# One block of sixteen of the first attention pass fetched by one-hot products; the second relational sum waits for the group it reads

## The chip, the cores and the metric

The kernel runs on one NeuronCore of a Trainium2 chip. The metric is device time in microseconds (us) of the whole program, lower is better. Five engines work side by side, each through its own list of instructions in order: TensorE (PE; its weight loads are shown as PEld), VectorE (DVE), ScalarE (ACT), GpSimd (POOL) and SyncE (SP), the last here only to issue DMAs. They meet through semaphores.

## The reference, cut to what matters

Four graph layers follow one another on 3125 nodes with 128 features and 100000 edges sorted by destination. Every layer is preceded by a layer norm with relu and added to `x`. The change touches the first layer, a graph attention with 8 heads, and the sum of the second layer (with which the edge half of the fourth is computed):

```python
# layer 0: attention over the incoming edges of each node
xl = (x @ W).reshape(N, 8, 16)
a_src, a_dst = (xl * att_src).sum(-1), (xl * att_dst).sum(-1)
e = leaky_relu(a_src[src] + a_dst[dst], 0.2)
ex = exp(e - segment_max(e, dst)[dst])
alpha = ex / (segment_sum(ex, dst)[dst] + 1e-16)
out = segment_sum(alpha[:, :, None] * xl[src], dst)

# layer 1, applied twice: a weight per relation
H = einsum("ni,rio->nro", x, einsum("rb,bio->rio", comp, V))
agg = segment_sum(H[src, etypes] * norm, dst)
```

So each edge needs the row of its source node: 128 features of `xl` and 8 numbers `a_src` in layer 0, and 128 features of its (node, relation) pair in layer 1.

## The kernel before

The edges, in order of destination, are cut into blocks of 128, two blocks to a "super" (391 supers). Destinations are cut into 25 tiles of 128 nodes. A step is one super for one tile; a super that straddles two tiles gets a step for each, so there are 415 steps, padded to 416. `ntile` and `estep`, computed on the chip, hold each step's tile and super. Four steps make a set, so there are 104 sets (`SETS`) of 8 blocks.

**The first attention pass**, `stage_gat` (calls from L653 on). POOL fetches one row of the table `tab0` (136 floats: `xl` and `a_src`) for each edge of a block with one indirect DMA, eight to a set, 832 in all (L691), into a ring `G` of `RG` = 12 sets; it may overwrite a set's place once DVE has weighted it (`y_done`). The iteration s of the main loop does this:

- ACT: `onehots(s+1)`, two operations over 1024 columns (L702, L705) on the destination numbers that SP has loaded to all partitions (`load_dst`, L657), giving the transposed one-hot matrix `MT`; `copy_weights(s-8)` (L713); one small step of the softmax (`step_of`: one of four steps in turn, so that four sets make one chunk of the softmax).
- PE: `score_products(s)` (L904, 8 products of 8 columns, each with a weight load of 128), `sums(s-8, 0)` (L947), the softmax step's transposes (L918 to L934), `sums(s-8, 1)`. The sums of a step go to one of `RS` = 5 PSUM banks.
- DVE: the softmax step (`masks`, `scans`, `chain`, `maxima`), `weigh(s-8)` (one-hots at L847, the product with the gathered rows at L855), `add_up(s-9)` (L840), `scores(s)` (L870, L873), which waits for the landing of all gathers of set s.

`LAG` = 8 sets lie between the scores and the weighted sums of a set. PE, ACT and DVE release each other within an iteration; POOL is only held by the ring. SP stands in its own queue: after two `load_dst` come three loads of single columns (L667 to L671), the first keys (L662), loads for a neighbouring stage (`aside.loads`), then `load_dst(2)` and so on.

**The last sum**, `stage_last_sum`, is not changed but has been using the method that the change brings to the first pass: one block in eight isn't fetched by POOL. Its source numbers are loaded to all partitions; for each of the 25 node tiles, ACT (two operations, L1111 and L1120) or DVE (one, L1165) builds a one-hot matrix of 128 nodes by 512 edges, PE multiplies it by the table's tile and adds up the 25 products (L1193), and the result, turned by four transposes (L1200), is copied into the ring.

**The second relational sum**, `stage_edges` (L477 on). POOL gathers 98 groups (`GROUPS_N`) of 8 blocks (L503, 782 gathers, the last group has 6) into a ring of 16 groups. PE makes the edge features (`features`, L535) and the sums (L555 for the gathered rows, L559 for the features), DVE adds them up (L595), ACT does relu and weights. Groups hold supers 4g to 4g+3, while set s holds steps 4s to 4s+3; because straddling supers take two steps, the super of a step falls behind the step's number, by 24 at the end. Before the change PE waits at set s < 98 for all of group s (`full[s % RG]`) whichever group its steps read.

## Time and profile before

| | us |
|---|---|
| three runs | 5646.87, 5653.91, 5638.48 |
| their median | 5646.87 |
| the profiled execution | 5653.79, of it 5652.1 in the span of the core |
| `stage_gat`, first gather to the last addition | 53.6 to 1178.5 |
| `stage_edges`, first gather to the last addition | 2356.7 to 3379.7 |
| `stage_last_sum`, first gather to the last | 4717.8 to 5586.2 |

| engine | busy over the span |
|---|---|
| POOL | 3887.6 us (69%) |
| PE | 3821.5 us (68%) |
| DVE | 2680.4 us (47%) |
| ACT | 2032.5 us (36%) |

Five of the program's stages are rows of indirect DMAs on POOL, one after the other. The busy share of an engine over the span tells little, since what an engine costs depends on the stage; the stretches of a stage and the waits within it have to be read. PE's clock is granted at one of two levels, 1.2 and 2.4 GHz, shown as 0.50 and 1.00; a mean between them is a mixture. The profiled execution is 6.9 us above the median of the three runs.

### The profile page before, as it was taken

The numbers are of one execution on the slowest core, as the hardware profiler recorded it, in microseconds if no ns is written. First come the engines' busy times: TensorE is split into PE (matmuls) and PEld (weight loads), VectorE is DVE, ScalarE is ACT, GpSimd is POOL, SyncE is SP. The second block draws the span as 40 slices with busy tenths as digits, with TensorE's granted clock in tenths as the row PEclk, the third lists the DMA queues.
The fourth block names the chain that finished last, engine by engine and source line by source line (L and its number), as shares of the span: only waits on it lengthen the run. The fifth ranks groups of instructions, "written<-read, shape, count | busy, mean of one in ns | idle before, by whom it ended". The sixth has DMA issues, their size and how long they took to land. (4 is left out here: it accounts for less than half of the span.)

```text
span 5652.1 us, 74589 instructions
## 1 busy us (share of the span) xinstructions
PE 3821.5 (68%) x20008; PEld 3215.9 (57%) x20008; DVE 2680.4 (47%) x8891; ACT 2032.5 (36%) x4370; POOL 3887.6 (69%) x4031
## 2 busy tenths in 40 slices
PE   3677777764533333777777776666676776988885
PEld 3676677743433333577777774665566663555554
DVE  4566666673222222433343344777777764332222
ACT  2222222220000000233333334566556636766663
POOL 6777777707777777477777744777777734777774
PEclk6555555577656556777777787999999988999997
DMA  4333334323222111422222215565665612222221
GB/s 124 108 108 105 108 107 110 100 89 106 53 54 52 52 52 52 140 60 60 60 60 60 60 39 161 159 160 158 160 159 158 159 50 65 62 60 60 60 58 42
DMA packets 393967, 515.71 MB, mean 91 GB/s; under 512 B 103179, under 2 KB 279138, under 8 KB 393178
## 3 DMA queue, kind: packets, MB, share of 16 engines
q0 software_dynamic: 128128, 265.50, 18.9%
q1 hardware_dynamic: 262745, 245.10, 14.5%
q8 instruction: 177, 2.90, 0.2%
q14 instruction: 228, 1.86, 0.1%
q10 hardware_dynamic: 2689, 0.36, 0.1%
HBM read 466.63 MB, written 43.94 MB: 90 GB/s over the span
## 5 line engine op out<-in xcount | busy, mean ns | idle before, releaser
L1696 POOL DMA_INDIRECT arena<-tab_x,idx_a x880 | 833.0, 947 | 314.5 <-issue 267.7
L996 POOL DMA_INDIRECT arena<-tab_rel,idx_b x782 | 761.8, 974 | 390.9 <-issue 238.2
L691 POOL DMA_INDIRECT arena<-tab,idx_a x832 | 821.0, 987 | 259.6 <-issue 252.5
L503 POOL DMA_INDIRECT arena<-tab_rel,idx_b x782 | 743.3, 951 | 267.9 <-issue 238.1
L1097 POOL DMA_INDIRECT arena<-tab_h,idx_a x686 | 660.5, 963 | 269.0 <-issue 208.5
L1037 PE MATMUL PS<-arena,att 128*128 x1664 | 359.4, 405 | 594.8 <-DMA arena<-tab_rel,idx_b 579.1
L1037 PEld LDWEIGHTS PS<-arena,att 128*128 128x128 f32 x1664 | 335.9, 309 | 619.4 <-issue 619.3
L1014 DVE TENSOR_SCALAR att<-iota_row,drel,wgt 128x128 f32<-128x128 f32 x832 | 222.9, 366 | 694.0 <-PE PS L1037 693.9
L1193 PE MATMUL PS<-arena,H 128*128 128x512 f32 x1200 | 538.6, 603 | 11.0 <-ACT arena L1134 11.0
L595 DVE TENSOR_TENSOR arena<-arena,PS 128x128 f32 x832 | 240.5, 289 | 601.5 <-PE PS L559 526.6
L555 PE MATMUL PS<-arena,att 128*128 x1664 | 372.2, 365 | 223.3 <-DMA arena<-tab_rel,idx_b 210.7
L947 PE MATMUL PS<-att,arena 128*128 128x136 f32 x1664 | 426.3, 435 | 62.1 <-issue 53.9
L555 PEld LDWEIGHTS PS<-arena,att 128*128 128x128 f32 x1664 | 323.5, 272 | 242.2 <-issue 241.4
L947 PEld LDWEIGHTS PS<-att,arena 128*128 128x128 f32 x1664 | 382.6, 325 | 70.0 <-issue 59.0
L1878 DVE SCALAR_TENSOR_TENSOR arena<-arena,att,PS 128x129 f32 x880 | 307.1, 349 | 215.4 <-issue 80.8
L1797 ACT ACTIVATE arena<-arena,att 128x128 f32<-128x128 f32 x880 | 281.2, 390 | 330.5 <-DVE att L1866 330.4
L1753 PE MATMUL PS<-arena 128*128 128x129 f32 x1760 | 267.3, 296 | 194.6 <-ACT arena L1789 194.6
L904 PEld LDWEIGHTS PS<-arena 128*128 128x128 f32 x1664 | 358.9, 325 | 56.5 <-issue 56.5
L904 PE MATMUL PS<-arena 128*128 x1664 | 348.0, 347 | 54.6 <-ACT arena L705 41.7
L1193 PEld LDWEIGHTS PS<-arena,H 128*128 128x128 f32 x1200 | 228.8, 196 | 273.1 <-issue 236.8
L1165 DVE TENSOR_SCALAR arena<-arena 128x512 f32<-128x512 int32 x192 | 101.1, 527 | 558.8 <-PE PS L1193 554.1
L1753 PEld LDWEIGHTS PS<-arena 128*128 128x128 f32 x1760 | 223.5, 198 | 250.5 <-ACT arena L1789 250.5
(389 smaller groups left out, 7209.9 us busy)
## 6 DMA issues: line engine op xcount, KB each, us to landing
arena<-pair_d SPq DMA_DIRECT2D x220, 256.0 KB
arena<-tab_u SPq DMA_DIRECT2D x880, 64.0 KB
arena<-drel_rows SPq DMA_DIRECT2D x104, 512.0 KB
tab_rel<-arena SPq DMA_DIRECT2D x50, 512.0 KB
arena<-tab_rel,idx_b POOLq DMA_INDIRECT x1564, 2.5
arena<-tab_x,idx_a POOLq DMA_INDIRECT x880
arena<-tab,idx_a POOLq DMA_INDIRECT x832
arena<-tab_h,idx_a POOLq DMA_INDIRECT x686
```

The costliest lines, as they stand in the source:

```text
L503: pool.indirect_dma_start(out=G[:, o:o + D], out_offset=None, in_=table, in_offset=bass.IndirectOffsetOnAxis(ap=idx_row[:, c:c + 1], axis= ...
L555: nc.tensor.matmul(PS[:, b:b + D], MW[s % 2][:, k * P:(k + 1) * P], G[:, bass.ds(e * (2 * D) + g * D, D)], start=(g == 0), stop=(g == 1))
L691: pool.indirect_dma_start(out=G[:, o:o + 136], out_offset=None, in_=tab0, in_offset=bass.IndirectOffsetOnAxis(ap=idx_src[:, 8 * s + k:8 * ...
L904: ins = nc.tensor.matmul(B7[:, k * 8:k * 8 + 8], MT[s % 2][:, k * P:(k + 1) * P], ad[:, bass.ds(tiles[k // 2] * 8, 8)], start=True, stop=True)
L947: ins = nc.tensor.matmul(PS[:, b:b + W], M[s % 2][:, k * P:(k + 1) * P], Y[s % 2][:, k, :, :].rearrange("p h c -> p (h c)"), start=(g == 0 ...
L996: pool.indirect_dma_start(out=G[:, o:o + D], out_offset=None, in_=table, in_offset=bass.IndirectOffsetOnAxis(ap=idx_row[:, c:c + 1], axis= ...
L1037: ins = nc.tensor.matmul(acc, M[s % RM][:, k * P:(k + 1) * P], G[:, bass.ds(e * (2 * D) + g * D, D)], start=False, stop=True, skip_group_c ...
L1097: pool.indirect_dma_start(out=G[:, o:o + D], out_offset=None, in_=table, in_offset=bass.IndirectOffsetOnAxis(ap=idx_last[:, c:c + 1], axis ...
L1193: nc.tensor.matmul(BANK, H[:, c * D:(c + 1) * D], SEL[i % NS], start=(c == 0), stop=(c == NT - 1)).then_inc(pick_done, 1)
L1696: pool.indirect_dma_start(out=G[:, o:o + D], out_offset=None, in_=tab_x, in_offset=bass.IndirectOffsetOnAxis(ap=idx_pair[:, 4 * g + u:4 * ...
L1753: ins = nc.tensor.matmul(PS[:, b:b + W], PB_[g % 2][:, u * P:(u + 1) * P], G[:, o:o + W], start=True, stop=True)
L1878: dve.scalar_tensor_tensor(a, a, ff[g % 8][:, u:u + 1], PS[:, b:b + W], ALU.mult, ALU.add).then_inc(acc_done, 1)
```

## The change

In `stage_gat`, from set 8 on, the last block of every second set (s odd, `picked(s)`) is no longer gathered: 48 blocks, one of sixteen, so POOL issues 784 gathers. Four such blocks (512 edges) of eight sets are made together, one quad ahead. In iteration s of an eight, up to four of the 25 node tiles are dealt with (4, 4, 4, 4, 4, 4, 1, 0): ACT builds the one-hot matrix for 17 of the 25 tiles with `distance` and `select`, DVE for 8, in one of four buffers `SEL`, and PE multiplies it by the table's tile in `X` after the iteration's sums (`pick`). In the eighth iteration ACT copies the result out of PSUM (`rows_out`), PE turns it (`turn`), ACT copies it again (`rows_back`), and `row_in(s+2)` puts a block in its place in the ring. DVE computes that block's `a_src` itself in `scores`, with a product and a reduction. There are 12 quads and 300 picks.

The table stays in `X`: at the end of `stage_begin` ACT copies `xl` there, and SP loads `x` back at the end of `stage_gat`. The buffers `SEL` and `SRC` lie in `H`, which SP first stores to `tab_h` and loads back at the end. PSUM bank 4 goes to the picks, so `RS` is 4. The source numbers are stored in `src_rows` by `stage_begin`.

In `stage_edges` POOL announces each group's landing through one counter, `landed`: after the third gather of group g it waits until group g-1 has landed and adds one. PE waits at set s for the number of groups that its last step needs, `need[s] = (estep[4s+3] >> 2) + 1`, computed on DVE.

```diff
@@ stage_edges
+                            if g and c == 8 * g + 2:
+                                pool.wait_ge(full[(g - 1) % RG], 128 * ((g - 1) // RG + 1))
+                                pool.sem_inc(landed, 1)
+                    last = GROUPS_N - 1
+                    pool.wait_ge(full[last % RG], 128 * (last // RG) + 16 * (2 * ST - 8 * last))
+                    pool.sem_inc(landed, 1)
...
+                        groups = load_need(mybir.EngineType.PE, need, s)
                         pe.wait_ge(r_done, s + 1)
                         pe.wait_ge(w_done, s + 1)
-                        if s < GROUPS_N:
-                            pe.wait_ge(full[s % RG], 128 * (s // RG) + 16 * min(8, 2 * ST - 8 * s))
+                        pe.wait_ge(landed, groups)
@@ stage_begin, ACT and SP
+                    sp.dma_start(src_rows.rearrange("(b p) e -> p b e", p=JB),
+                                 sl[1][0:JB, :].rearrange("p (b e) -> p b e", b=4)).then_inc(s_rows, 16)
...
+                    act.wait_ge(s_ev, 7)
+                    nc.scalar.copy(v3(X[:]), tab[:, :, 0:D])
@@ stage_gat
-            RS, W = 5, 136
+            RS, W = 4, 136
...
+            def picked(s):
+
+                return s >= 8 and s % 2 == 1
...
+            def chunks(s):
+
+                q, v = s // 8 + 1, s % 8
+                return [(q, c) for c in range(min(4 * v, NT), min(4 * v + 4, NT))] if q < QUADS else []
@@ stage_gat, SP
                     load_key(0)
                     load_key(1)
+                    sp.dma_start(tab_h.rearrange("(t p) f -> p t f", p=P), v3(H[:])).then_inc(s_keep, 16)
+                    sp.wait_ge(s_keep, 16)
+                    load_src(1)
+                    load_src(2)
                     aside.loads(sp)
                     for s in range(2, SETS):
                         sp.wait_ge(mt_done, s - 1)
                         load_dst(s)
+                        if s % 8 == 1 and 3 <= s // 8 + 1 < QUADS:
+                            q = s // 8 + 1
+                            sp.wait_ge(sel_act, NA * (q - 2))
+                            sp.wait_ge(sel_dve, ND * (q - 2))
+                            load_src(q)
...
                     aside.stores(sp)
+                    sp.wait_ge(pick_done, NT * (QUADS - 1))
+                    sp.wait_ge(sel_act, NA * (QUADS - 1))
+                    sp.dma_start(v3(X[:, 0:(NT - 1) * D]), node_view(t["x"], True)).then_inc(s_keep, 16)
+                    sp.dma_start(X[0:NLAST, (NT - 1) * D:NW], node_view(t["x"], False)).then_inc(s_keep, 16)
+                    sp.dma_start(v3(H[:]), tab_h.rearrange("(t p) f -> p t f", p=P)).then_inc(s_keep, 16)
+                    sp.wait_ge(s_keep, 64)
@@ stage_gat, POOL
-                        for k in range(8):
+                        for k in range(7 if picked(s) else 8):
@@ stage_gat, ACT
+                    def distance(j):
+
+                        q, c = j // NA + 1, ACT_TILES[j % NA]
+                        if j % NA == 0:
+                            act.wait_ge(s_src[q % 2], 16 * ((q + 1) // 2))
+                        if j >= 2:
+                            act.wait_ge(sel_act, j - 1)
+                        nc.scalar.activation(DIST[j % 2], SRC[q % 2], ACT.Abs, bias=away[:, c:c + 1]
+                                             ).then_inc(dist_done, 1)
+
+                    def select(j):
+
+                        i = NT * (j // NA) + ACT_TILES[j % NA]
+                        act.wait_ge(dist_done, j + 1)
+                        if i >= NS:
+                            act.wait_ge(pick_done, i - NS + 1)
+                        nc.scalar.activation(SEL[i % NS], DIST[j % 2], ACT.Relu, bias=ones[:, 0:1], scale=-1.0
+                                             ).then_inc(sel_act, 1)
@@ stage_gat, DVE
                     def scores(s):
...
+                        if picked(s):
+                            n = s // 2 - 3
+                            dve.wait_ge(made, n)
+                            dve.tensor_tensor(WS, g[:, 7, 0:D], asb, ALU.mult).then_inc(s_ws, 1)
+                            dve.wait_ge(s_ws, 2 * n - 1)
+                            dve.tensor_reduce(g[:, 7, D:D + 8], WS.rearrange("p (h c) -> p h c", c=16), AX_X, ALU.add
+                                              ).then_inc(s_ws, 1)
+                            dve.wait_ge(s_ws, 2 * n)
@@ stage_gat, PE
+                    def pick(q, c):
+
+                        i = NT * (q - 1) + c
+                        if c in DVE_TILES:
+                            pe.wait_ge(sel_dve, ND * (q - 1) + DVE_TILES.index(c) + 1)
+                        else:
+                            pe.wait_ge(sel_act, NA * (q - 1) + ACT_TILES.index(c) + 1)
+                        if c == 0 and q > 1:
+                            pe.wait_ge(freed, q - 1)
+                        nc.tensor.matmul(BANK, X[:, c * D:(c + 1) * D], SEL[i % NS], start=(c == 0), stop=(c == NT - 1)
+                                         ).then_inc(pick_done, 1)
...
                         if s >= LAG:
                             sums(s - LAG, 1)
+                        if s < SETS:
+                            for q, c in chunks(s):
+                                pick(q, c)
+                            if s % 8 == 7 and s // 8 + 1 < QUADS:
+                                turn(s // 8 + 1)
```

What this makes of the order is seen on two engines. PE, the end of an iteration of `stage_gat` and the start of the next, before (L918 is the softmax step's transposes, the sums are L947, the score products L904):

```order
L904 MATMUL PS<-arena 128x8 x2
L947 MATMUL PS<-att,arena 128x136 x4
L918 MATMUL PS<-ident,HT 128x128 x2
L947 MATMUL PS<-att,arena 128x136 x4
L136 TENSOR_LOAD ntile
```

and after, where the same operations have the lines L1055, L1098 and L1069:

```order
L1055 MATMUL PS<-arena 128x8 x2
L1098 MATMUL PS<-att,arena 128x136 x4
L1069 MATMUL PS<-ident,HT 128x128 x2
L1098 MATMUL PS<-att,arena 128x136 x4
L1112 MATMUL PS<-H,X 128x512 x4
L144 TENSOR_LOAD ntile
```

Four picks (L1112) now stand between the second half of the sums and the next iteration's score products.

ACT, one such iteration before, from the one-hots of the next set on (`onehots`, `copy_weights`, the softmax step's copy, then the next set's one-hots):

```order
L702 ACTIVATE arena<-arena,pidx 128x1024
L705 ACTIVATE arena<-arena,ones 128x1024
L713 COPY att<-att 128x64
L726 COPY att<-PS 128x256
L702 ACTIVATE arena<-arena,pidx 128x1024
L705 ACTIVATE arena<-arena,ones 128x1024
```

and after:

```order
L781 ACTIVATE arena<-arena,pidx 128x1024
L784 ACTIVATE arena<-arena,ones 128x1024
L792 COPY att<-att 128x64
L845 COPY att<-PS 128x256
L801 ACTIVATE extra<-H,extra 128x512 x2
L810 ACTIVATE H<-extra,ones 128x512
L801 ACTIVATE extra<-H,extra 128x512
L810 ACTIVATE H<-extra,ones 128x512 x2
L781 ACTIVATE arena<-arena,pidx 128x1024
L784 ACTIVATE arena<-arena,ones 128x1024
```

Three `distance` (L801) and three `select` (L810) now stand behind the softmax step's copy and ahead of the next one-hots.

## Rows read from the trace of the kernel before

**Rows 1.** Page, groups: xcount | busy us, mean ns | idle before, releaser.
```profile
L691 POOL DMA_INDIRECT arena<-tab,idx_a x832 | 821.0, 987 | 259.6 <-issue 252.5
...
L1097 POOL DMA_INDIRECT arena<-tab_h,idx_a x686 | 660.5, 963 | 269.0 <-issue 208.5
```

**Rows 2.** Busy time by stretch: us, busy us of each engine (instructions), granted clock, DMA share.
```profile
60.00:1120.00 1060.00, 760.41 (x3405) 723.98 (x3405) 630.97 (x2249) 283.09 (x401) 809.93 (x821) 0.51 0.40 109
2400.00:3300.00 900.00, 692.85 (x4316) 665.23 (x4314) 355.05 (x1440) 303.41 (x891) 681.46 (x718) 0.77 0.23 60
4750.00:5500.00 750.00, 676.43 (x2584) 399.86 (x2584) 232.37 (x880) 531.79 (x800) 569.77 (x592) 0.95 0.23 60
```

**Rows 3.** Waits in `stage_gat`, 200 to 1120 us: total us, times, longest us.
```profile
POOL arena L691 <- issue: 216.2, 709, 0.3
DVE att L870 <- DMA arena<-tab,idx_a: 209.2, 76, 4.9
...
POOL arena L691 <- DVE att L855: 0.9, 3, 0.3
```

**Rows 4.** Timeline of PE in `stage_gat`: start us, us, line, what, number.
```profile
615.35 3.42 PE L904 MATMUL PS<-arena 128*128 x16
...
623.43 2.18 PE L947 MATMUL PS<-att,arena 128*128 128x136 f32 x8
```

**Rows 5.** The last sum: PE in the timeline, then groups on ACT and DVE.
```profile
4764.90 7.03 PE L1193 MATMUL PS<-arena,H 128*128 128x512 f32 x16
...
L1111 ACT ACTIVATE arena<-arena 128x512 f32<-128x512 int32 x408 | 294.3, 722 | 30.9 <-DMA arena<-in_src 17.8
L1120 ACT ACTIVATE arena<-arena,ones 128x512 f32<-128x512 f32 x408 | 289.6, 710 | 139.6 <-PE PS L1193 139.6
...
L1165 DVE TENSOR_SCALAR arena<-arena 128x512 f32<-128x512 int32 x192 | 101.1, 527 | 558.8 <-PE PS L1193 554.1 <-DMA arena<-in_src 4.7
```

**Rows 6.** The last sum: a wait on PE in the timeline, and the clock.
```profile
5111.03 3.78 PE L1226 MATMUL PS<-arena,att 128*128 x16 [4.83 <-DMA arena<-tab_h,idx_a]
...
5112.00:5116.00 4.00, 4.00 (x16) 0.50 0.20 53
5116.00:5118.00 2.00, 2.00 (x6) 1.00 0.27 70
```

**Rows 7.** Timeline of POOL and DVE in `stage_gat`.
```profile
657.94 1.98 POOL L691 DMA_INDIRECT arena<-tab,idx_a  x1 [0.30 <-issue]
...
658.15 1.64 DVE L847 TENSOR_SCALAR arena<-iota_row,drel 128x128 f32<-128x128 f32 x8
```

**Rows 8.** The start of `stage_gat` on SP and ACT; a store of a table.
```profile
82.80 16.21 SPq L657 DMA_DIRECT2D arena<-drel_rows  x5
...
90.00 1.15 ACT L702 ACTIVATE arena<-arena,pidx 128x1024 f32<-128x1024 f32 x1 [28.26 <-DMA arena<-drel_rows]
...
tab<-arena SPq DMA_DIRECT2D x1, 1700.0 KB, 7.6
```

**Rows 9.** Timeline of `stage_edges`: a landing, then the end of the stage.
```profile
2707.03 1.01 POOL L503 DMA_INDIRECT arena<-tab_rel,idx_b  x1 [0.30 <-issue]
...
2709.97 1.22 PE L555 MATMUL PS<-arena,att 128*128 x4 [2.93 <-DMA arena<-tab_rel,idx_b]
...
3333.36 0.94 POOL L503 DMA_INDIRECT arena<-tab_rel,idx_b  x1 [0.30 <-issue]
...
3337.11 0.95 POOL L503 DMA_INDIRECT arena<-tab_rel,idx_b  x1 [0.30 <-issue]
...
3340.65 0.86 PE L555 MATMUL PS<-arena,att 128*128 x4 [2.33 <-DMA arena<-tab_rel,idx_b]
...
3348.03 0.71 PE L555 MATMUL PS<-arena,att 128*128 x4
...
3353.78 0.71 PE L555 MATMUL PS<-arena,att 128*128 x4
...
3378.99 0.72 DVE L595 TENSOR_TENSOR arena<-arena,PS 128x128 f32 x2 [0.21 <-DVE arena L595]
```

More of the change, by code:

```diff
@@ L46 @@
 assert NB + TN - 1 <= PR and PR % 4 == 0
+GATHERS = -(-ST // 4)
 FAR, FLOOR = 2.0 ** 60, 2.0 ** 58
@@ L88, in build @@
         estep = sb("estep", [1, SS], I32)
+        extra = sb("extra", [P, 1216])
         att = sb("att", [P, K * 8])
@@ L117, in build @@
         EW = small[0:17, 0:D]
+        asb, node, away = extra[:, 0:D], extra[:, D:D + NT], extra[:, D + 32:D + 32 + NT]
+        DIST = [extra[:, 192 + 512 * i:704 + 512 * i] for i in range(2)]
+        ACT_TILES = [c for c in range(NT) if c % 3 < 2]
+        DVE_TILES = [c for c in range(NT) if c % 3 == 2]
+        NA, ND = len(ACT_TILES), len(DVE_TILES)
         def v3(ap, n=D):
@@ L138, in load_tiles, with needed_groups, load_need @@
             return values
+        def needed_groups(dve, row, done):
+            dve.tensor_scalar(row, estep[:, 3::4], 2, None, ALU.arith_shift_right).then_inc(done, 1)
+            dve.wait_ge(done, 1)
+            dve.tensor_scalar(row, row, 1, None, ALU.add).then_inc(done, 1)
+        def load_need(eng, row, s):
+            return nc.values_load(row[0:1, s:s + 1], engines=[eng], min_val=1, max_val=GATHERS)
         class Chain:
```

96 lines of the change are left out of this document (75 added, 21 removed).

## The prediction

> **What bounds the kernel now.** I first read the busy shares and the costliest groups of the page. Three groups of indirect DMAs on POOL head the list [rows 1]; of them L691 belongs to `stage_gat` and L1097 to the last sum. The table by stretches then says what else is full in each stage [rows 2], and the list of waits says who waits for whom in `stage_gat` [rows 3]: POOL's longest wait between 200 and 1120 us is 0.3 us of its own issue, it waited for DVE three times for 0.9 us in all, and DVE waited 209.2 us for gathers. So POOL sets the pace there, at (821.0 + 252.5) / 832 = 1.290 us a gather [rows 1], or 10.3 us a set, and PE, DVE and ACT follow. PE is the second: busy for 760.41 of 1060 us, but at a granted clock of 0.51, that is at 1.2 GHz nearly always [rows 2]. An iteration's parts on PE show it: 3.42 us of score products and two halves of sums of 2.2 us [rows 4].
>
> **The gathers that go.** 48 gathers at 1.290 us are **-61.9 us**, if POOL still sets the pace. For that, eight sets have to fit into 60 x 1.290 = 77.4 us on each other engine; before, they had 64 x 1.290 = 82.6 us.
>
> PE, per eight sets: 760.41/1060 x 82.6 = 59.3 us at clock 0.51, or 30.2 us of work at the full clock. The 25 picks are added. In the last sum eight picks (16 instructions) take 7.03 us at the full clock [rows 5], 0.88 us each, so 22.0 us; the four transposes of a turn add about 0.6. Together 52.8 us at the full clock, so the time that PE needs is **52.8/g**, with g the granted clock: 106 us at 0.50, 77.4 us at 0.68. Here lies the decision. The trace has both outcomes: `stage_edges` with 693 of 900 us busy has 0.77, the last sum with the same picks 0.95 [rows 2], this stage with much the same busy share 0.51. The picks stand in a row behind the second half of the sums, a burst of 2.2 + 4 x 0.88 to 4 x 1.76 us, and such a burst is what raised the clock in the last sum: after 4.83 us of waiting PE worked at 0.50 until about 5116 us and from then on at 1.00 [rows 6]. Every iteration but the last two of eight has such a burst. Once PE falls behind POOL it waits for nothing, and the bursts come closer. I take g = 0.70 to 0.75, so 70 to 75 us.
>
> The page "TensorE: Matmul & The Clock Gate" of the Trainium skill, section "HAM oscillation — how this bites in real kernels", speaks against the change: bursts of products between waits let the clock fall again each time, so that each burst starts cold. By it g would stay near 0.5 and the stage be bound by PE; this is rival C below, whose price comes from rows. The trace bears out the falling (4.83 us of waiting, then 0.50) [rows 6], yet also that a long burst ends at the full clock.
>
> DVE, per eight sets: 630.97/1060 x 82.6 = 49.2 us, plus 8 compares of 0.527 us [rows 5] = 4.2, plus four times a product and a reduction of 128 x 128 with their hand-overs. Nearest is L840's kind of row at 0.3 us and 0.2 us between; I take 1.0 us a time, 4.0. Together 57.4 of 77.4. ACT: 283.09/1060 x 82.6 = 22.1, plus 17 x (0.722 + 0.710) = 24.3 [rows 5], plus about 2.3 for copies, 48.7 of 77.4. Both fit on their own. But the engines hand over within an iteration: PE's picks come before the next score products, for which DVE's `scores` waits, for which PE's softmax step waits. At the full clock this round is 0.5 + 0.4 + 1.1 + 3.5 + 1.9 = 7.4 us (halves of [rows 4] and four picks), at the low one 13.4 us, against 9.7 us that POOL takes for a set. In softmax steps 0 and 3 ACT starts its selects only after PE's transposes: 3 x 1.43 + 0.4 + 0.9 = 5.6 us instead of 4.6. The ring absorbs some iterations that are late: it is four sets (about 38 us) deeper than the lag. I take **+8 us** for stalls of POOL that the ring doesn't absorb; bounds are 0 and 37 us (rival B's T). `RS` = 4 makes the first sum of a set wait for an addition that DVE makes 0.3 to 1.2 us after `weigh`; it lies in the same slack, at nothing.
>
> DVE's added compares stand beside POOL's gathers. One gather took 1.98 us and ended with the eight compares of L847 that began 0.2 us after it [rows 7]. But L1097, with 192 such 512-wide compares beside it, has a mean of 963 ns, L691 has 987 without them [rows 1]. I take **+3 us**. The page "SBUF — State Buffer" of the Trainium skill, section with the "DVE blocks DMA" trap, says that a DVE operation in a two-port mode locks GpSimd out of its port while it makes descriptors; by it each of 96 compares could cost its 0.527 us, 51 us in all, and the sum would be -24 instead of -72.
>
> **Start, end and the stages beside.** SP issued `load_dst(2)` at 82.80 us and its one-hots began at 90.00 [rows 8]. Ahead of it now come the store of `H` (a store of 1700 KB took 7.6 us [rows 8]), a wait for it and two source loads: some 10 us. The first picks, and PE behind them, wait for this too, to about 95 us. POOL first needs the others at set 12, at 53.6 + 96 x 1.26 = 174 us, when iteration 8 must have weighted set 0; from 109 us, seven iterations at 7 to 9 us lead there by 172 us at the latest, since the last two of an eight have one pick or none. So nothing, with 15 us as the upper bound. At the end SP reloads 3.2 MB, some 15 us by the same row, beside the last two sets' gathers; the tail of the stage (DVE, to 1178.5 us) starts from the last landing. **+3 us**, bounds 0 and 8. The copy of 3200 columns to `X` in `stage_begin` (some 3.5 us on ACT, idle there) and the extra store are covered by DVE's work to 51 us and the store of `tab0`: nothing, 3.5 without that cover.
>
> **The wait for the group.** In `stage_edges` POOL sets the pace too, and PE waits for each landing. After the last one PE starts set 97 at 3340.65 and DVE ends the stage at 3378.99 + 0.72 = 3379.71: 39.1 us for seven sets, of which six are only waiting in line, at 5.75 us each (3348.03 to 3353.78) [rows 9]. From the reference's `dst` I worked out `need`: up to set 39 it is the set's own group, set 100 reads to group 95, sets 101 and 102 to 96, set 103 to 97. Group 96 is announced after the third gather of group 97, at 3333.36 + 0.94 = 3334.30. Then sets 101, 102, 103 follow in 39.1 - 4 x 5.75 = 16.1 us, to 3350.4; group 97 has landed by then. That is **-29.3 us**. The pipeline that hides the earlier sets is there: PE was idle 2 to 3 us in each.
>
> The price is POOL's: 97 waits and additions, with all later gathers queued behind each. The wait itself is free as long as a group lands before the third gather after it ends, 3 x 1.25 = 3.75 us; the lags read are 2709.97 - 2708.04 = 1.9 us and 3340.65 - 3338.06 = 2.6 us [rows 9]. The additions cost between nothing (the gathers that carry a wait have the same 0.3 us before them as all [rows 3]) and 0.30 us each, 29 us. I take 0.05 us, **+5 us**, nearer to the row of the waiting gathers. Sets up to 39 start some 1.8 us later than their landing, which nobody waits for.
>
> **The sum.** -61.9 + 8 + 3 + 3 - 29.3 + 5 = -72.2 us. On the profiled execution 5653.8 that gives 5581.6; it lies 6.9 us over the median, so against the median 5646.9 I predict **5575 us** (0.987).
>
> **Rivals.**
> A, the forecast: POOL keeps the pace, 5550 to 5598 (by the bounds of the small terms). For it: the last sum, same method, 0.95. Chance 0.56.
> B, PE and DVE share the bound, at g near 0.66 or by hand-overs: eight sets take about 80.5 us, 12 x 2.1 = 25 us are gained in place of 54, so 5604, 5598 to 5635. For it: no more than 2 us of slack a set. Chance 0.24.
> C, slower than before: the bursts do not keep the clock up. With g = 0.60 eight sets take 88 us, 12 x 5.4 = +65, plus 6 and minus 24 gives 5694; with g = 0.50 it is 106 us and 5910. It decides where 12 x (T - 82.6) exceeds 18, T = 84.1, g below 0.63. For it: 0.51 in this stage at 72% busy [rows 2]. Against it: bursts three times as long. Chance 0.12.
> D, the group's wait holds POOL: a lag over 3.75 us costs its excess 97 times, at 4.5 us +73, about 5648. Against it: 1.9 and 2.6. Chance 0.03.
> E, more than forecast: nothing of the +16 us of small terms comes true and fewer gathers are held, under 5550. Chance 0.05.
>
> **How the numbers follow.** The measurement tells about 0.3% (17 us) from no change. The range 5550 to 5640 leaves out C, D and E, 0.20. Faster by over 0.3% (below 5630): A, E and most of B, 0.82. Within 0.3%: the rest of B and D, 0.06. Slower: C, 0.12.
>
> **What would show it.** In the changed profile: 784 gathers in the stage with idle time before them put down to issue alone (A) or to DVE's weighting (B, C); the granted clock in the stage over 0.68 (A), under 0.63 (C); picks of 0.88 us; the mean of a gather under 1.0 us; the end of `stage_edges` some 12 us after the last gather instead of 42, with 0.30 us before the fourth gather of a group as before. The prediction is wrong if POOL's gathers stretch, or if the round of hand-overs is longer than 9.7 us at the full clock as well.

## The result and the profile after

The changed kernel takes 5562.21 us (median of 4 runs, 5556.26 to 5566.20), the kernel before beside it 5649.54 us: a ratio of 0.9847, interval 0.9832 to 0.9862, 87 us less. A second set of runs gave 5566.48 against 5652.07 us, 0.9853 (0.9836 to 0.9869). The forecast was 5575 us, 72 us less. One thing is needed to read some of the numbers below: in three of the five sets of experiments all kernels, the one before among them, ran at a slower pace (7007 to 7038 us instead of 5648 for the kernel before), which has a section of its own.

The profiled execution has a span of 5562.5 us. Its page, costliest groups, as in [rows 1]; and then two groups that are new, the picks on PE and the compares on ACT:

```profile
L770 POOL DMA_INDIRECT arena<-tab,idx_a x784 | 775.9, 990 | 244.7 <-issue 238.0 <-POOLq L70 6.1 <-DVE att L985 0.6
...
L529 POOL DMA_INDIRECT arena<-tab_rel,idx_b x782 | 741.0, 948 | 266.9 <-issue 233.8 <-POOLq L70 28.8 <-DMA arena<-tab_rel,idx_b 4.0
...
L1112 PE MATMUL PS<-H,X 128*128 128x512 f32 x600 | 318.8, 671 | 93.1 <-ACT H L810 90.6 <-DVE H L996 2.5
...
L801 ACT ACTIVATE extra<-H,extra 128x512 f32<-128x512 f32 x204 | 138.8, 715 | 33.5 <-DMA H<-src_rows 31.9
```

L770 are the gathers of `stage_gat`: 784 in place of 832, with 238.0 us of their own issue between them, 6.1 us ahead of the first, and 0.6 us of waiting for DVE. The pace is (775.9 + 238.0) / 784 = 1.293 us a gather, where it was 1.290.

The table by stretches for `stage_gat` and `stage_edges`, as [rows 2] (columns as there):

```profile
60.00:1060.00 1000.00, 823.82 (x4041) 626.06 (x4041) 689.51 (x2434) 560.02 (x881) 764.75 (x773) 0.81 0.44 120
...
2400.00:3300.00 900.00, 702.81 (x4584) 674.28 (x4584) 382.84 (x1507) 321.88 (x943) 664.20 (x702) 0.79 0.23 59
```

In `stage_gat` POOL's share is what it was (76%), ACT's has doubled (56% against 27%), and PE's and DVE's have grown by ten points each (82% against 72%, 69% against 60%). PE's granted clock is 0.81 where it was 0.51. The waits of the stage between 200 and 1060 us, as [rows 3]:

```profile
POOL arena L770 <- issue: 201.4, 661, 0.3
...
DVE att L1018 <- PE PS L1055: 57.7, 32, 4.8
...
PE PS L1098 <- DVE arena L970: 40.3, 28, 6.0
...
DVE att L1018 <- DMA arena<-tab,idx_a: 11.9, 4, 5.3
POOL arena L770 <- DVE att L985: 0.6, 2, 0.3
```

DVE used to wait 209.2 us for landings [rows 3]; now it waits 11.9 us for them and 57.7 us for PE's score products. PE, DVE and ACT run behind the gathers instead of on their heels: DVE's scores start some 20 us, or two sets, behind the last gather of their set in the first half of the stage, and some 4 us at its end. The ring of twelve sets takes up the difference, and POOL is not held. PE's wait of 40.3 us for DVE's additions (L970) is new. It does not come from PE's greater share, for the kernel without picks (below), which has `RS` = 4 too, shows more of it, 95.5 us:

```profile
PE PS L1082 <- DVE arena L957: 95.5, 54, 8.6
```

The kernel before, with `RS` = 5, had 2.7 us of it in the whole stage. POOL does not pay for it.

The two traces laid beside each other by the first gather of each stage (us from the span's start):

| first gather of | before | after | difference |
|---|---|---|---|
| `stage_gat` | 53.6 | 53.3 | -0.3 |
| first relational sum | 1280.8 | 1222.5 | -58.3 |
| `stage_edges` | 2356.7 | 2298.8 | -57.9 |
| attention | 3464.2 | 3374.4 | -89.8 |
| last sum | 4717.8 | 4631.1 | -86.7 |
| end of the span | 5652.1 | 5562.5 | -89.6 |

So `stage_gat` gave 58 us, `stage_edges` 32, and each of the others is within some 3 us of nothing. The end of `stage_edges` in the timeline, to be read beside [rows 9] (start us, us, engine, line):

```profile
3276.90 0.94 POOL L529 DMA_INDIRECT arena<-tab_rel,idx_b  x1 [0.30 <-issue]
...
3279.46 0.71 PE L587 MATMUL PS<-arena,att 128*128 x4
...
3283.19 0.71 PE L587 MATMUL PS<-arena,att 128*128 x4
...
3287.72 0.72 DVE L628 TENSOR_TENSOR arena<-arena,PS 128x128 f32 x2 [0.21 <-DVE arena L628]
```

The last gather starts at 3276.90, PE starts the last two sets at 3279.46 and 3283.19, and DVE is done at 3287.72 + 0.72 = 3288.44: 11.5 us behind the last gather. Before it was 3379.71 - 3337.11 = 42.6 us, with seven sets in line [rows 9].

### The profile page after: what moved, and what is told of

Read it like the earlier page. It is cut to its first block and busy times, and to the rows that moved or that the text cites. A ratio compares the mean times of both kernels' runs of the same rounds, so it can differ in the third digit from the quotient of the medians.

```text
span 5562.5 us, 77284 instructions
## 1 busy us (share of the span) xinstructions
PE 3866.2 (70%) x20656; PEld 3101.8 (56%) x20656; DVE 2741.3 (49%) x9085; ACT 2312.9 (42%) x4851; POOL 3836.1 (69%) x3983
## 5 line engine op out<-in xcount | busy, mean ns | idle before, releaser
L1171 POOL DMA_INDIRECT arena<-tab_rel,idx_b x782 | 761.9, 974 | 392.6 <-issue 238.0
L770 POOL DMA_INDIRECT arena<-tab,idx_a x784 | 775.9, 990 | 244.7 <-issue 238.0
L1212 PE MATMUL PS<-arena,att 128*128 x1664 | 358.1, 404 | 597.1 <-DMA arena<-tab_rel,idx_b 581.4
L1212 PEld LDWEIGHTS PS<-arena,att 128*128 128x128 f32 x1664 | 334.4, 308 | 621.8 <-issue 621.8
L587 PE MATMUL PS<-arena,att 128*128 x1664 | 362.0, 357 | 208.9 <-POOLq L535 183.7
L587 PEld LDWEIGHTS PS<-arena,att 128*128 128x128 f32 x1664 | 313.3, 264 | 227.4 <-issue 225.8
L1112 PE MATMUL PS<-H,X 128*128 128x512 f32 x600 | 318.8, 671 | 93.1 <-ACT H L810 90.6
L548 ACT ACTIVATE arena<-PS 128x512 f32<-128x512 f32 x208 | 112.9, 594 | 638.5 <-PE PS L567 638.5
L1330 DVE TENSOR_SCALAR arena<-arena,extra 128x512 f32<-128x512 int32 x192 | 99.0, 516 | 558.3 <-PE PS L1358 553.3
L1098 PE MATMUL PS<-att,arena 128*128 128x136 f32 x1664 | 319.6, 352 | 75.7 <-DVE arena L970 58.5
L1918 PEld LDWEIGHTS PS<-arena 128*128 128x128 f32 x1760 | 226.0, 200 | 247.4 <-ACT arena L1954 247.4
```

The lines of the kernel that those rows point to most:

```text
L587: nc.tensor.matmul(PS[:, b:b + D], MW[s % 2][:, k * P:(k + 1) * P], G[:, bass.ds(e * (2 * D) + g * D, D)], start=(g == 0), stop=(g == 1))
L770: pool.indirect_dma_start(out=G[:, o:o + 136], out_offset=None, in_=tab0, in_offset=bass.IndirectOffsetOnAxis(ap=idx_src[:, 8 * s + k:8 * ...
L1098: ins = nc.tensor.matmul(PS[:, b:b + W], M[s % 2][:, k * P:(k + 1) * P], Y[s % 2][:, k, :, :].rearrange("p h c -> p (h c)"), start=(g == 0 ...
L1112: nc.tensor.matmul(BANK, X[:, c * D:(c + 1) * D], SEL[i % NS], start=(c == 0), stop=(c == NT - 1)).then_inc(pick_done, 1)
L1171: pool.indirect_dma_start(out=G[:, o:o + D], out_offset=None, in_=table, in_offset=bass.IndirectOffsetOnAxis(ap=idx_row[:, c:c + 1], axis= ...
L1212: ins = nc.tensor.matmul(acc, M[s % RM][:, k * P:(k + 1) * P], G[:, bass.ds(e * (2 * D) + g * D, D)], start=False, stop=True, skip_group_c ...
```

## Experiments

### The first part alone

`stage_edges` is as it was before; everything else is the changed kernel.

```
-                        groups = load_need(mybir.EngineType.PE, need, s)
...
-                        pe.wait_ge(landed, groups)
+                        if s < GROUPS_N:
+                            pe.wait_ge(full[s % RG], 128 * (s // RG) + 16 * min(8, 2 * ST - 8 * s))
```

> The changed kernel with stage_edges as it was: PE waits again for the gathers of its own group, POOL announces nothing. If the two parts of the change stand in different stages and simply add, as the two traces suggest (stage_gat 57.9 us shorter, stage_edges 28.8 us shorter), this run gives 5562 + 29 = 5591 us, stage_edges takes its 980 us from first to last gather with 42 us behind it. Rival: the announcements cost POOL part of what they save (5 us in the prediction's sum); then POOL's gathers in stage_edges are shorter here by that, and the run comes out at 5586 or lower.

5592.22 us, ratio 0.9902 (0.9886 to 0.9919). Last gather and last addition in `stage_edges`:

```profile
L528 POOL DMA_INDIRECT arena<-tab_rel,idx_b x782: 940/944/1068, 2298.6 to 3277.2; - x196
...
3318.09 0.72 DVE L620 TENSOR_TENSOR arena<-arena,PS 128x128 f32 x2 [0.21 <-DVE arena L620]
```

The gathers run from 2298.6 to 3277.2 as in the changed kernel, and the tail is 3318.09 + 0.72 - 3277.2 = 41.6 us again. The second part is worth 30 us, and all of it lies behind the last gather.

### The second part alone

The kernel before, with the new `stage_edges` and its two helpers.

```
+                            if g and c == 8 * g + 2:
+                                pool.wait_ge(full[(g - 1) % RG], 128 * ((g - 1) // RG + 1))
+                                pool.sem_inc(landed, 1)
...
+                        groups = load_need(mybir.EngineType.PE, need, s)
...
+                        pe.wait_ge(landed, groups)
```

> The kernel before with only stage_edges changed: PE waits for the group that its set reads. Adding parts give 5649 - 29 = 5620 us, stage_gat unchanged at 1.290 us a gather and a granted clock of 0.51. Rival: the first part of the change also helped stage_edges (its start, its clock); then less than 29 us is gained here.

5621.38 us, ratio 0.9948 (0.9931 to 0.9964), with a granted clock of 0.51 in `stage_gat` as before. 0.0098 and 0.0052 saved apart make 0.0150; together it was 0.0153, and the intervals are some 0.0016 wide to either side. Within that the parts add, and neither helps the other.

### What the announcements cost POOL

The 97 waits and additions stay in POOL's queue, but PE waits for its own group.

```
-                        pe.wait_ge(landed, groups)
+                        if s < GROUPS_N:
+                            pe.wait_ge(full[s % RG], 128 * (s // RG) + 16 * min(8, 2 * ST - 8 * s))
```

> The changed kernel, with POOL's 97 waits and additions kept in stage_edges, but PE waiting for its own group as before: POOL's price alone, against the run with only the first part. The prediction's sum has 5 us for it, bounds 0 and 29. The trace after shows 978.1 us from first to last gather against 980.4 before, so the theory now is 0 to 2 us: 5591 us. By the rival (0.30 us for each addition) 5620 us.

5593.35 us, 0.9903 (0.9886 to 0.9919), 1.1 us over the first part alone, which is well inside the interval. The trace of the changed kernel shows one announcement (an answer on its line: duration min/median/max in ns, first and last start), and who waits for it:

```profile
L535 POOLq EVENT_SEMAPHORE  x97: 17/17/17, 2310.3 to 3271.9; - x97
...
  PE PS L587: 183.7, 74
```

17 ns each, 1.6 us in all. The 4.0 us for which the page lets POOL wait for its own landings are 13 gathers with 0.3 us ahead of them, the gap that every gather has. The last stands at 3271.9, before POOL's engine begins the third gather of group 97 (3273.16): the queue that holds the wait runs a gather ahead of the engine that moves the data. I had reckoned with the end of that third gather, 3273.16 + 0.94 = 3274.10; the announcement comes 2.2 us earlier, 1.6 us behind the end of the group's last gather.

### No picks at all

The 48 gathers stay out, and so do picks, turns, distances and selects. A unit matrix is copied where the picked rows would stand, so the work of fetching these rows is left out on every engine.

```
-                        mine = act_chunks(s)
...
-                                pick(q, c)
...
-                        nc.scalar.copy(G[:, o:o + D], ROWS_T[:, u * P:(u + 1) * P]).then_inc(made, 1)
+                        nc.scalar.copy(G[:, o:o + D], ident[:]).then_inc(made, 1)
```

> The changed kernel without picks, turns, distances and selects; the 48 gathers are still left out, and a unit matrix is copied where the picked row would be, so these rows are wrong. If POOL alone sets the pace of stage_gat (theory), it takes the same 1.29 us a gather, and the whole time is that of the changed kernel within 5 us (5557 to 5567); PE's granted clock in the stage falls back to 0.5 to 0.6. If PE or DVE shared the bound, the stage gets shorter by up to 30 us. If DVE's added compares slowed POOL's gathers (3 us in the sum, up to 51 us by the port lock), their mean of 990 ns falls: at 963 ns 21 us less.

5560.42 us, ratio 0.9843 (0.9827 to 0.9859): the same as with the picks, to 2 us. Its page, its stretch and two of its waits:

```profile
L769 POOL DMA_INDIRECT arena<-tab,idx_a x784 | 778.3, 993 | 244.8 <-issue 235.6 <-POOLq L70 6.2 <-DVE att L972 3.0
```

```profile
60.00:1060.00 1000.00, 708.66 (x3385) 672.08 (x3385) 650.39 (x2329) 292.22 (x449) 765.30 (x771) 0.55 0.44 120
```

```profile
POOL arena L769 <- issue: 198.7, 652, 0.3
...
DVE att L1005 <- DMA arena<-tab,idx_a: 126.2, 42, 5.4
```

Three things follow. All that the picks add (some 320 us on PE, 280 on ACT, 45 on DVE) is hidden behind POOL's gathers. The picks are what lifts the granted clock: 0.55 without them, 0.81 with them, at the same pace of the stage. Whether it is their work, the row in which they stand, or the waits that they fill, this run doesn't tell. And DVE's added compares do not slow the gathers: their mean is 993 ns without the compares and 990 with them. By the Trainium skill (page "SBUF — State Buffer", the section with the "DVE blocks DMA" trap) a compare that runs in a two-port mode would lock POOL out of the shared port for as long as it runs. These runs show none of it: 96 compares of 495 ns would be 48 us, and the two kernels differ by 2. In which mode the compares run is not shown.

### The row of picks broken up, one gather more left out, the picks doubled

Three kernels ask what holds the clock up, how much room the other engines have, and how the stage answers to more PE work. The first moves an iteration's picks one iteration later and splits them:

```
                             score_products(s)
+                            late = chunks(s - 1) if s else []
+                            for q, c in late[0:2]:
+                                pick(q, c)
...
                             sums(s - LAG, 0)
+                        if s < SETS:
+                            for q, c in late[2:]:
+                                pick(q, c)
...
-                            for q, c in chunks(s):
-                                pick(q, c)
```

> The changed kernel with the picks of an iteration no longer in one row behind the second half of the sums: they come one iteration later, two behind the score products and two behind the first half of the sums. The work is the same, the burst is broken. If it is the long burst that holds the granted clock up (as the prediction argues), the clock in stage_gat falls from 0.81 to under 0.65 and the kernel is slower by 50 us or more. If it is how much work PE has in all (busy 824 of 1000 us against 709 without the picks), the clock stays at 0.75 to 0.85 and the time at 5562 us within 6.

The second leaves out one gather more of each odd set from set 12 on (rows of an earlier set stand in its place):

```
-                        for k in range(7 if picked(s) else 8):
+                        for k in range(gathers(s)):
...
+            def gathers(s):
+                return 8 if not picked(s) else 6 if s >= RG else 7
```

> The changed kernel with one more gather left out of each odd set from set 12 on (46 of them), and nothing made in its place: rows of an earlier set are used there, so the output is off. POOL's pace becomes 56 gathers or 72.2 us for eight sets. If the other engines have slack (PE busy 64 of 77.4 us at a clock of 0.81, DVE 53), the kernel gains 46 x 1.290 = 59 us more: 5503 us. If the round of hand-overs is nearly as long as POOL's 9.7 us a set, POOL waits for DVE's weighting instead and less than half of that is gained: over 5530 us.

The third adds a product with a zero block to 22 picks of each eight sets:

```
+                        if c >= 3:
+                            nc.tensor.matmul(BANK, NIL, SEL[i % NS], start=False, stop=False)
```

> The changed kernel with 22 of the 25 picks of each eight sets preceded by a product of the same size with a zero block (the sum is unchanged): 264 x 0.88 = 232 us of work more for PE at the full clock. PE then needs (52.8 + 19.4)/g for eight sets: 76 us at a granted clock of 0.95, 85 at 0.85, 89 at 0.81. If more work also brings a higher clock, the stage lengthens little: 5562 to 5620 us, with the clock over 0.88. If the clock stays at 0.81, 12 x 12 = 140 us more: 5700 us.

All three were measured at the slower pace, where the kernel before took 7037.76 us: 7049.76 us (1.0019, 1.0010 to 1.0028), 7045.21 us (1.0013, 1.0004 to 1.0022) and 7151.00 us (1.0168, 1.0149 to 1.0186). The first two were measured once more:

> The kernel with the picks spread over the iteration once more, since on the other chip PE's products came so slowly (7038 us for the kernel before) that POOL no longer set the pace and the question stayed open. Where the kernel before takes its 5648 us: if the long burst holds the granted clock up, the clock in stage_gat falls from 0.81 to under 0.65 and the time is 50 us or more over 5562. If PE's work in all does it, the clock stays at 0.75 to 0.85 and the time at 5562 us within 6.

> The kernel with 46 more gathers left out (rows of an earlier set stand in their place, so the output is off) once more, for the same reason. Where the kernel before takes 5648 us: 5503 us if the other engines have the slack (POOL's pace 72.2 us for eight sets, against 64 us of PE and 53 us of DVE); over 5530 us, with POOL waiting for DVE's weighting, if the round of hand-overs is nearly as long as POOL's 9.7 us a set.

The pace was slow again, 7012.22 us for the kernel before: 7019.02 us (1.0015, 1.0006 to 1.0025) and 7005.85 us (0.9997, 0.9984 to 1.0009). None of the expectations in absolute numbers can be held against these. What can be compared are stages of kernels that ran in one set on one chip. The kernel with the changed sums, below, has the changed kernel's `stage_gat` unaltered, so it is the reference. First to last gather of `stage_gat`: 1457.7 us with the changed stage, 1410.2 with the picks spread, 1407.0 with 46 gathers less, 1503.6 with the picks doubled. Measured once more, the first three took 1426.6, 1392.2 and 1365.5 us, the reference on another chip. The reference's profiled execution was 27 us above its median, so the medians are a second guide: the whole times differ from 7134.7 - 41 us (the reference less what its changed sums cost, below) by -44, -48 and +57 us.

- One gather more left out per odd set: 50.7 us for 46 gathers, 1.10 us each (61.1 us when measured again). POOL waits for DVE's weighting for 486.8 us there and for 474.9 in the reference, yet most of a gather's price comes back: the stage is held by the others in some stretches and by POOL in the rest. How much room the others have at the usual pace was not measured.
- Doubled picks: 264 products of 0.88 us, 232 us at the full clock, cost 45.9 us. The rest was covered. The granted clock from 210 to 1410 us was 0.80 against 0.72.
- Spread picks: the stage is 47.5 us shorter than with the picks in a row, and 34.4 us when measured again. The clock of the stage, of the spread kernel and then of the reference:

```profile
210.00:1410.00 1200.00, 829.01 (x3640) 607.02 (x3640) 627.62 (x2219) 502.25 (x794) 636.80 (x660) 0.73 0.29 81
```

```profile
210.00:1410.00 1200.00, 793.45 (x3524) 583.03 (x3525) 609.25 (x2165) 493.85 (x775) 612.45 (x632) 0.72 0.29 78
```

0.73 with the picks spread, 0.72 with them in a row (0.75 and 0.73 when measured again), where I had expected under 0.65 or 0.75 to 0.85 at the usual pace. So a row of four picks is not needed for the clock, as far as this pace can show it. But the run doesn't part the amount of PE's work from how long PE works without a wait, because the spread picks fill the places between its other products. In the spread kernel PE works from 600.06 to 617.13 us with picks among its products and no wait:

```profile
600.06 0.69 PE L1085 MATMUL PS<-ident,att 128*128 128x128 f32 x2 [9.53 <-DVE att L1018]
...
605.62 3.76 PE L1112 MATMUL PS<-H,X 128*128 128x512 f32 x4
...
615.17 1.96 PE L1112 MATMUL PS<-H,X 128*128 128x512 f32 x4
619.39 1.22 PE L1098 MATMUL PS<-att,arena 128*128 128x136 f32 x8 [2.26 <-DVE arena L970]
```

What is shown is that the clock rises and falls with the picks: 0.51 and 0.55 without them, 0.81 with them, and 0.80 against 0.72 with them doubled, at the slower pace. Which property of the added work does it stays open. Whether the spread kernel would also be faster at the usual pace, where POOL leaves nothing to win, is open too.

### The same wait in the other two sums

In the changed kernel PE still has seven sets in line behind the last landing of the first relational sum (15.45 us) and of the last sum (14.55 us). This kernel gives both stages POOL's announcements and PE's wait for the group that the set reads:

```
+                            if g and c == 8 * g + 2:
+                                pool.wait_ge(full[(g - 1) % RG], landed_count(g - 1))
+                                pool.sem_inc(landed, 1)
...
+                        groups = load_need(mybir.EngineType.PE, need, s)
...
-                        if s < GROUPS_N:
-                            pe.wait_ge(full[s % RG], 16 * sum(gathers(g) for g in range(s % RG, s + 1, RG)))
+                        pe.wait_ge(landed, groups)
```

> The changed kernel with the same wait (for the group that the set reads, announced by POOL) in the first relational sum and in the last sum too. There PE still works through seven sets in 15.45 and 14.55 us behind the last landing. With the wait only the last set or two are left: about 13 us less in each of the two stages, at nothing on POOL: 5536 us. Rival: the announcements or the load of the value cost PE or POOL something (0.02 us for each of 195 additions, 4 us), or DVE's one-hots come no earlier, so that under 10 us are gained: over 5552 us.

> The kernel whose first relational sum and last sum also wait for the group that the set reads, once more. The slower runs showed what the load of that value costs PE: 0.65 to 0.80 us ahead of each set where PE stands in a row with work and nothing covers it. Where the kernel before takes 5648 us, PE waits for landings in both stages and the load is covered, save in the last sets: seven sets in 15.45 and 14.55 us behind the last landing become one or two, about 12 us less in each stage, so 5538 us (ratio 0.9805). Rival: the load is not covered, 208 x 0.7 us on PE's path, and the time is over 5600 us.

Both times at the slower pace: 7134.66 us against 7037.76 (1.0142, 1.0122 to 1.0163) and 7122.20 against 7007.08 (1.0167, 1.0153 to 1.0181). Two prices show. The first is POOL's. First to last gather of the first sum took 1180.4 us, beside 1150.1, 1145.4 and 1147.9 of the three kernels of the same set: 30 us more. POOL lost them at the start of the stage, at the first two announcements:

```profile
1741.93 0.95 POOL L1172 DMA_INDIRECT arena<-tab_rel,idx_b  x1 [29.97 <-DMA arena<-tab_rel,idx_b]
...
1760.11 0.95 POOL L1172 DMA_INDIRECT arena<-tab_rel,idx_b  x1 [8.32 <-DMA arena<-tab_rel,idx_b]
```

These are the 12th and the 20th gather, each the first behind an announcement. SP has just issued a load of 6250 KB (`in_attr`) there, and the first groups land late; that the load is the reason is likely, but no run leaves it out. With the waits in its queue POOL stands still until they have landed, 29.97 + 8.32 us, of which a later wait for the ring pays back some; the second measurement has 29.91 and 8.29 us. The late landing is there at the usual pace too. In the changed kernel, whose POOL doesn't wait, the first gather starts at 1222.48 and PE's first set at

```profile
1267.96 3.77 PE L1212 MATMUL PS<-arena,att 128*128 x16 [29.40 <-DMA arena<-tab_rel,idx_b]
```

This is rival D of the prediction, a landing that comes later than the announcement can bear, in a stage for which I had not asked it. In `stage_edges` the announcements hold POOL at neither pace: even at the slower one all its pauses of over 0.6 us stand before the first gather of a group, where it waits for the ring.

The second price is PE's. What follows the last gather of the last sum took 99.7 us beside 89.4, 93.0 and 88.7. The last sum's PE in this kernel, and then in the one with the spread picks:

```profile
7077.75 2.05 PE L1411 MATMUL PS<-arena,att 128*128 x16 [0.68 <-issue]
...
7080.44 2.05 PE L1411 MATMUL PS<-arena,att 128*128 x16 [0.64 <-issue]
...
7083.28 2.05 PE L1411 MATMUL PS<-arena,att 128*128 x16 [0.80 <-issue]
```

```profile
6973.75 25.99 PE L1395 MATMUL PS<-arena,att 128*128 x208
```

Thirteen sets in one row of 25.99 us without the load; with it 0.64 to 0.80 us of idle time ahead of each set of 2.05 us. The load's own instructions in PE's queue nearly account for it:

```profile
L156 PEldq TENSOR_LOAD <-HT x312: 305/309/317, 1707.5 to 7107.1; - x156
L156 PEldq FUSED_REGOPS  x312: 151/151/165, 1707.8 to 7107.5; - x156
L156 PEldq SEQ_ASSERT  x312: 18/18/28, 1708.1 to 7107.7; - x156
```

They take 0.48 us a set, 0.60 with the gaps between them, behind the two loads that each set had already. Where PE waits for something else this is hidden: in the changed `stage_edges` the last two sets follow each other without a gap (3279.46 and 3283.19 us, 3.7 us of products each). Whether the last sum would gain its 12 us at the usual pace was not measured. For the first sum an estimate from the rows above is a loss: the wait behind gather 11 alone would hold POOL from about 1236 to 1267 us, more than the 12 us that its end could give.

### The slower pace

The changed kernel itself, as a reference for these numbers:

> The changed kernel itself, as the reference for the slower runs. Built up from them: the run with six gathers (7006 us) plus the difference of stage_gat between it and a kernel whose stage_gat is the changed one (1426.6 against 1365.5 us from first to last gather), 7067 us, where the kernel before took 7007 to 7012: slower by 0.8%. Where the kernel before takes 5648 us instead, 5562 us (0.985). Rival for the slower case: the change keeps its gain of 48 gathers there too, ratio under 0.995.

It came at the usual pace and repeated the result (5566.48 us, 0.9853); so the changed kernel was never measured at the slower one. Two views of the kernel with the spread picks show what the slower pace looks like. PE in `stage_edges`, and the waits of the whole span:

```profile
2994.07 0.37 PE L567 MATMUL PS<-small,arena 17*128 17x128 f32 x1 [3.13 <-issue]
2997.57 0.37 PE L567 MATMUL PS<-small,arena 17*128 17x128 f32 x1 [3.13 <-issue]
3000.38 0.37 PE L587 MATMUL PS<-arena,att 128*128 x1 [2.44 <-issue]
3002.47 0.37 PE L587 MATMUL PS<-arena,att 128*128 x1 [1.73 <-issue]
```

```profile
PEld PS L1216 <- issue: 698.4, 452, 30.5
...
PE PS L1216 <- issue: 601.3, 407, 15.1
...
POOL arena L770 <- DVE att L985: 434.7, 59, 45.2
```

For stretches of up to 150 us PE starts one product every 1.4 to 3.5 us, waiting for nothing that the profile shows, and DVE and ACT stand still behind it. A gather's median is 944 to 952 ns as ever. POOL therefore no longer sets the pace of the stage: it waits 434.7 us for DVE's weighting, where it waited 0.6 us. What holds PE's queue was not found. The pages of both paces have the same 184 and 236 packets on the two queues that carry instructions, at 0.2 and 0.1% of the span, so they give no sign of slow code loading. The same chip had both paces at different times.

What the change would do there can only be put together, from three sides. The run with six gathers plus the difference of `stage_gat` to a kernel with the changed one (1426.6 - 1365.5, two chips): 7067 against 7012 us. The changed sums, less the 30 and 11 us that they cost: 7134.7 - 41 = 7094 against 7038 us; and in the second measurement 7122.2 - 46 = 7076 against 7007 us (there the first sum took 35 us more). All three say 0.8 to 1.0% slower. That is an estimate, not a measurement. With the picks spread the kernel was measured at 0.2% slower than before, the better of the two there.

## Why the prediction was right, and where it was not

- **POOL keeps the pace** (forecast, rival A): right. 784 gathers, idle time put down to issue alone, 1.293 us each. First to last gather: 1127.1 - 53.6 = 1073.5 us before, 1066.9 - 53.3 = 1013.6 now, -59.9 against a term of -61.9.
- **PE's need, 52.8/g**: the work was right. 823.82/1000 of eight sets' 77.6 us is 63.9 us at a clock of 0.81, or 51.8 us at the full clock. A row of four picks took 3.60 us where it ran at the full clock. The clock was taken too low, 0.70 to 0.75. I derived it from the row of picks, and that reason is not borne out: spreading the row did not lower the clock (0.73 against 0.72, at the slower pace only), while leaving the picks out did (0.55, at the usual pace). That error went the forecast's way: with 0.70 to 0.75 PE would have had 2 to 7 us to spare in eight sets, and it had nearly 14. By the Trainium skill (page "TensorE: Matmul & The Clock Gate", section "HAM oscillation — how this bites in real kernels") bursts between waits would fall back to the low clock each time. The trace of the changed kernel does not show that pattern. The clock does fall, as at 606 us, but there PE had been busy for 7.19 of the 8 us before, and it then stays low while PE hardly waits (busy for 13.57 of 14 us). These are the two iterations of eight with one pick or none:

```profile
606.00:620.00 14.00, 13.57 (x60) 12.38 (x58) 11.62 (x42) 2.48 (x6) 10.65 (x12) 0.51 0.37 112
620.00:640.00 20.00, 17.48 (x91) 12.96 (x91) 12.08 (x46) 17.30 (x29) 15.43 (x16) 0.91 0.42 114
```

  The stage as a whole had 0.81, and rivals B and C, which needed 0.66 and under 0.63, did not come about. From one iteration's score products to the next's at the full clock it took 638.99 - 631.69 = 7.30 us, where I had 7.4:

```profile
629.01 2.84 PE L1112 MATMUL PS<-H,X 128*128 128x512 f32 x6 [0.24 <-ACT H L810]
631.69 1.85 PE L1055 MATMUL PS<-arena 128*128 x16
...
638.99 1.85 PE L1055 MATMUL PS<-arena 128*128 x16
```

- **Stalls of POOL, +8**: 0.6 us of waits in the whole stage. This term was mis-sized. The iterations that ran at the low clock between 602 and 632 us lasted 8.3 to 12.4 us, but those at the full clock get back 9.7 - 7.3 = 2.4 us each, and the ring covers what is between.
- **DVE beside the gathers, +3**: the mean rose from 987 to 990 ns, 2.4 us in all, and was 993 without the compares. The number was right by luck; the reason was not.
- **Start, 0**: right. The first pick starts at 95.15 us, where I had put it at about 95, and POOL did not feel it:

```profile
95.15 6.55 PE L1112 MATMUL PS<-H,X 128*128 128x512 f32 x8 [32.41 <-ACT H L810]
```

- **End of the stage, +3**: from the last gather to the first of the next stage 155.6 us against 153.7, +1.9.
- **DVE and ACT**: 689.51/1000 x 77.6 = 53.5 us and 560.02/1000 x 77.6 = 43.5 us for eight sets, where I had 57.4 and 48.7. DVE's product and reduction took 0.6 us a time instead of 1.0.
- **The wait for the group, -29.3**: right. The tail shrank from 42.6 to 11.5 us, 31.1 less; the announcement comes 2.2 us earlier than I had it. The second part alone measured 27 us by the medians and 29 by the ratio, taking it away 30.
- **POOL's announcements, +5**: 17 ns each, 1.6 us; between the two runs 1.1 us. Mis-sized: the gathers that carry a wait were the right row, and I should have taken nothing. The bound that I gave for the wait, 3.75 us of lag, held in `stage_edges`; in the first sum, beside the large load, the same waits held POOL for 38 us.

The sum was -72.2 us, the result -87 and the difference of the two traces -89.6. Stretch by stretch, forecast and trace: first to last gather of `stage_gat` -61.9 + 8 + 3 = -50.9 and -59.9; its end +3 and +1.9; the tail of `stage_edges` -29.3 and -31.1; its gathers +5 and -2.3 (978.1 us against 980.4, a length that varies by 2 us between runs: 978.6 without announcements, 980.3 with them). The two large terms were right to 2 us each. The four small terms with a plus were +19 in the sum (rival E has them as +16); in the traces stalls and DVE together came to +2.0, the end to +1.9 and POOL's gathers in `stage_edges` to -2.3. Most of what was missed lies there. They were margins and not readings, each with a row in the trace of before that would have carried a smaller value.

## What to carry to other kernels

- Where an engine's queue of gathers sets a stage's pace, each gather that another engine can make instead is worth nearly its full pitch (here 59.9 us for 48, 1.25 us each at a pitch of 1.29), as long as the others' work for the same sets fits into the rest, counted at the clock that they will have with the added work.
- A stage that hands its results on in fixed order should wait for the data that it reads, not for the data with its own number: the line behind the last transfer goes. Two prices have to be looked up first: whether a large load beside the gathers makes them land late (then an announcement in the gathers' own queue holds the gathers), and whether the waiting engine has time in its queue for the value that says how far to wait.
- Both parts were won on slack of PE, and slack is what changes first: at another pace of the same chip the same kernel would lose 0.8 to 1.0%, by the estimate above.

## What the runs showed of the hardware

- More work for PE came with a higher clock: from 716 to 824 us busy in 1000, the granted clock rose from 0.51 to 0.81, and the old work took less time. The median of a score product's instruction fell from 361 to 256 ns.
- An addition to a semaphore in POOL's queue takes 17 ns, and the queue is up to one gather ahead of POOL's engine.
- Beside a load of 6250 KB issued by SP, gathers issued by POOL landed tens of microseconds late: with a wait for them in its queue POOL stood still for 29.97 and 8.32 us, where `stage_edges` shows landings 1.6 us behind the gather's end.
- The same kernel on the same chip took 5648 us at one time and 7012 us at another, with PE starting its products late and a gather's median unchanged at 944 to 952 ns.
- Where a row of sets of 2.05 us left PE's queue no slack, one more register load a set (0.48 us of instructions) cost 0.64 to 0.80 us a set.
